# A mean-embedding projection on one Trainium2 core: tiles of users join the sweep over the weights three loads earlier

## What is computed

```python
valid = sequence_ids < emb_table.shape[0]          # ids 1024 x 200, table 12500 x 512
safe_ids = jnp.where(valid, sequence_ids, 0)
seq_emb = emb_table[safe_ids]
seq_emb = seq_emb * valid[..., None].astype(seq_emb.dtype)
denom = jnp.maximum(valid.sum(axis=1, keepdims=True).astype(seq_emb.dtype), 1.0)
user_repr = seq_emb.sum(axis=1) / denom
logits = user_repr @ proj_w + proj_b               # 512 x 12500, in fp32
```

## Time and profile before

| | |
|---|---|
| median of 3 runs | 706.61 us (704.24 to 707.12) |
| the profiled execution | 707.86 us, its span 706.1 us |
| TensorE busy | 638.2 us, 90% |
| VectorE, GpSimd, ScalarE busy | 396.0, 233.3, 147.6 us |
| granted TensorE clock, mean | 0.956 of full speed |
| DMA | 156.24 MB, mean 221 GB/s |
| read from HBM, written | 113.66 MB, 51.20 MB |
| chain that ended last | PE 76%, issue 9%, DVE 6%, DMA 4% |
| joins (first unit of tiles 1 to 7) | units 10, 22, 35, 51, 65, 81, 98 |

### The profile page before, as it was taken

The page is one execution under the profiler, slowest core; times in us unless marked ns, Lnnn a source line. Parts: engine busy times, 40 slices in busy tenths (PEclk is TensorE's granted clock), DMA queues, the critical chain, the costliest instruction groups (busy, mean ns, idle before and its releaser), DMA issues.

```text
span 706.1 us, 7456 instructions
## 1 busy us (share of the span) xinstructions
PE 638.2 (90%) x2627; PEld 491.2 (70%) x2627; DVE 396.0 (56%) x703; ACT 147.6 (21%) x173; POOL 233.3 (33%) x227
## 2 busy tenths in 40 slices
PE   1874797997989979987999999999999999999998
PEld 0323565765757747866878878888888888888886
DVE  7943843855937654967968754533333334434442
ACT  8402731623404202102002003211001111112110
POOL 6772747575663471763755400000000000000000
PEclk9985988999989988998999999999999999999999
DMA  9984987786876974985868816854545555566743
GB/s 316 357 256 121 336 307 223 248 295 213 288 217 187 313 251 156 299 258 175 313 220 267 296 73 206 285 171 162 165 146 174 161 186 167 165 219 193 211 146 109
DMA packets 75398, 156.24 MB, mean 221 GB/s; under 512 B 8007, under 2 KB 62738, under 8 KB 75354
## 3 DMA queue, kind: packets, MB, share of 16 engines
q1 hardware_dynamic: 58074, 108.25, 46.2%
q0 software_dynamic: 17280, 47.47, 22.0%
HBM read 113.66 MB, written 51.20 MB: 233 GB/s over the span
## 4 chain that ended last, share of the span: by engine, by line
PE 76%; issue 9%; DVE 6%; DMA 4%; ACT 2%; another core or an unknown queue 1%; POOLq 0%; POOL 0%; DVEq 0%; SPq 0%; ACTq 0%
PE acc L774 23%; PE acc L772 23%; PE acc L773 23%; PE turned L731 4%; DVE sums L522 3%; DMA rows<-in_L_rec_emb_table_dram,index 2%; DMA w_raw<-in_L_rec_proj_w_dram 1%; PE acc L776 1%; DVE w_lo L572 1%; PE turned L705 1%; PE turned L721 1%; ACT w_hi L398 1%; DVE mean L559 0%; DVE stage L584 0%
## 5 line engine op out<-in xcount | busy, mean ns | idle before, releaser
L772 PE MATMUL acc<-w_hi,mean_hi 128*128 128x500 f32 x800 | 328.9, 411 | 3.3 <-issue 3.1
L774 PE MATMUL acc<-w_hi,mean_lo 128*128 128x500 f32 x800 | 318.1, 398 | 1.2 <-issue 1.2
L773 PE MATMUL acc<-w_lo,mean_hi 128*128 128x500 f32 x800 | 316.2, 395 | 3.3 <-issue 3.2
L331 POOL DMA_INDIRECT rows<-in_L_rec_emb_table_dram,index x208 | 223.2, 1073 | 139.9 <-issue 71.9
L584 DVE TENSOR_TENSOR stage<-acc,bias_sb 128x500 f32<-128x500 f32 x149 | 100.6, 677 | 188.6 <-PE acc L774 178.7
L773 PEld LDWEIGHTS acc<-w_lo,mean_hi 128*128 128x128 f32 x800 | 154.3, 193 | 40.6 <-issue 8.5
L772 PEld LDWEIGHTS acc<-w_hi,mean_hi 128*128 128x128 f32 x800 | 154.4, 193 | 37.1 <-issue 8.1
L774 PEld LDWEIGHTS acc<-w_hi,mean_lo 128*128 128x128 f32 x800 | 153.5, 192 | 35.8 <-issue 4.4
L522 DVE SCALAR_TENSOR_TENSOR sums<-rows,mask,sums 128x512 f32<-128x512 f32 x159 | 119.6, 752 | 8.5
L398 ACT ACTIVATE w_hi<-w_raw 128x2000 fp32r<-128x2000 f32 x39 | 72.8, 1874 | 230.6 <-PE acc L774 210.8
L570 DVE TENSOR_TENSOR w_lo<-w_raw,w_hi 128x1000 fp32r<-128x1000 f32 x39 | 46.5, 1193 | 18.0 <-ACT w_hi L398 17.6
(11 more groups left out here) (92 smaller groups left out, 198.4 us busy)
## 6 DMA issues: line engine op xcount, KB each, us to landing
w_raw<-in_L_rec_proj_w_dram SPq DMA_DIRECT2D x39, 1000.0 KB
out_dram<-stage SPq DMA_DIRECT2D x72, 500.0 KB
out_dram<-stage SPq DMA_DIRECT2D x56, 250.0 KB
bias_sb<-in_L_rec_proj_b_dram SPq DMA_DIRECT2D x31, 250.0 KB
raw_at_hi<-in_L_rec_proj_w_dram SPq DMA_DIRECT2D x4, 1000.0 KB
raw_at_lo<-in_L_rec_proj_w_dram SPq DMA_DIRECT2D x4, 1000.0 KB
rows<-in_L_rec_emb_table_dram,index POOLq DMA_INDIRECT x208
ids_sb<-in_r_sequence_ids_dram SPq DMA_DIRECT2D x1, 700.0 KB, 4.6
```

Source lines behind the costliest of these rows:

```text
L331: return pool.indirect_dma_start(out=dst, out_offset=None, in_=table, in_offset=bass.IndirectOffsetOnAxis(ap=column, axis=0), bounds_check ...
L772: nc.tensor.matmul(bank, hi, high, start=k == 0, stop=False)
L773: nc.tensor.matmul(bank, hi, low, start=False, stop=False)
L774: last = nc.tensor.matmul(bank, lo, high, start=False, stop=k == K - 1 and r >= EARLY)
```

## The change

One line changes, the table of joins.

```diff
 def mean_embedding_projection(nc, ids, table, proj, bias, out, FAST=26,
-                              JOIN=(0, 10, 14, 17, 20, 22, 24, 26)):
+                              JOIN=(0, 7, 11, 14, 17, 19, 21, 23)):
```

## The result

The changed kernel takes 716.14 us (713.04 to 718.37, four runs), the kernel before, with one run more, 705.42 us. The ratio is 1.0139, with a 95% interval of 1.0102 to 1.0177: slower by 1.4%. I had forecast slower, 710.7 us against 706.61, which is 0.6%. The direction is right, the size, 4.1 us, is under half of the measured 10.7, and 716.14 lies 0.1 us over the upper end of the range. The profiled execution of the change took 718.37 us, 10.5 us more than that of the kernel before.

What follows compares the result with a forecast made beforehand. TensorE's units bound the last stretch; a chain of gathers, splits and waits bounds stage 1. Units +7.3 us less 3.2 us from an earlier join gave +4.1 us: 710.7 us against 706.61, range 701 to 716 us.

Steps and rivals of the forecast that it cites:

- The units at the end: Two more units in the last stretch cost 5.47 us, one more in stage 7 costs 1.85 us: together +7.3 us.
- what moves is the landing: Stage 1: TensorE's first gathered column lands 4.1 us sooner; with 0.86 us for a further sum, the join comes 3.2 us sooner.
- the middle of two bounds: TensorE's first column in stage 1 takes 5.9 us to land, between 4.40 and 7.38; join 4.7 to 1.7 us sooner.
- The further sum: Stage 1: the last gathers wait for two columns behind the split, not one, which costs 0.86 us.
- Stages 2 to 6 at nothing: Stages 2 to 6 keep their unit counts and cost nothing, covered by the 49 us each takes anyway.
- over 3 us in sum as a sign of being wrong: Stages 2 to 6 differing by more than 3 us in sum would mean their time is not the cadence read in it.
- the cadence rival: TensorE's signals come late in a long gather run across stage 1, eating the landing's gain: +7.3 us, 713.9; chance 0.16.
- Some 49 us whatever the count: Stages 2, 3, 5, 6 and 7, with 12 to 17 units, each take about 49 us regardless of units.
- The traffic: Rival: DMA traffic sets stage 1; gathers come 8.4 us sooner and 3.9 us of waiting goes: -5.0 us, 701.6; chance 0.24.
- The stage 4 load: Rival: VectorE's 5.71 us wait for a late load's split in stage 4 is on the path: -1.6 us, 705.0; chance 0.18.

Runs made afterwards that it cites:

- first pair: Traces of the kernel before and the change from the recorded result, 705.42 and 716.14 us, ratio 1.0139.
- second pair: Both kernels run again unchanged for their traces: the kernel before 661.42 us; the change 665.61 us against 661.12, ratio 1.0075.
- the kernel with more raw buffers: Kernel before with four raw buffers used up to load 18 in place of 15: 661.72 us against 660.56, ratio 1.0014.
- the joins from load 11: Kernel before with joins at loads 0, 11, 15, 18, 21, 23, 25, 27: 658.44 us, ratio 0.9963; with four raw buffers up to load 19, 654.91 us.

## Why the prediction was right and wrong

**The units at the end: right.** Forecast +7.3 us (5.47 and 1.85); measured +8.0 in the first pair of traces and in the second (2.4 and 5.6). The small rest is in stage 7, where 0.79 us of TensorE's waiting was still there with a unit more, so that only some 0.1 us of it was filled. The mean is made three units before the join and so moves with the units.

**Stage 1: the mechanism right, the number in part by luck.** The step "what moves is the landing" was forecast at 3.2 us by the middle of two bounds. In the second pair the join moved by 3.3 us. But TensorE's first column landed at 72.7 in place of 75.6, 2.9 us sooner and not 4.1. The further sum did cost what it should (4.69 us from the split to the last gathers in place of 3.84). The unit and the split behind the landing were 0.5 us faster, and the last two columns landed 0.8 us faster after their issue; neither was in the sum. And stage 1 of one order of work differs by 0.9 to 1.9 us from trace to trace. In the first pair the landing moved by 3.5 us, the mean by 3.7 and the join by 7.0; the other 3.3 us are the late take-up of the turning at 117.31, which the changed kernel had less of (ScalarE took it up at 110.79, and from the mean to the join it was 7.1 us and not 10.3).

**Stages 2 to 6 at nothing: the step that failed in the recorded result.** It measured +9.4 us in the first pair of traces, 7.1 of it in stage 2, and +0.5 in the second pair. The prediction had named over 3 us in sum as a sign of being wrong, and it came. In the first pair there are stops in which ScalarE takes up a finished unit 1.7 to 14.0 us late, in both kernels, at different places. In stage 2 they cost both kernels TensorE's waits at the turning and the list, the change 2.9 us more; the pauses between TensorE's matmuls, 2.4 us more, only lie beside such a stop. The forecast named late signals under the cadence rival and gave it 0.16. That rival's sum, +7.3, is nearer to the measured 10.7, but its place was not right: the loss ate the gain in stage 2, and not in stage 1. What causes the stops stays open. They are not a property of a long run of gathers, since the second pair has longer runs and none of them. Instruction loading is no likely cause either: the traces have 21 and 23 packets of it in both pairs.

**The reading behind it was wrong too.** "Some 49 us whatever the count" was taken from the first trace, and from a list that left out stage 4, with 58.89 us for 16 units. Where the signals came in time, stages 3 and 4 take 40.1 and 49.1 us for 13 and 16 units with TensorE busy throughout. There the cover of these stages was not a cadence but TensorE's own unchanged work, and the term was nothing for a different reason than the one I gave.

**The rivals.** The traffic (0.24) is refuted in its size: in the second pair the join came 3.3 us earlier, not 8.4. In the first it came 7.0 us earlier, and 3.2 of that is the waiting ahead of the join (3.9) which this rival had added. The stage 4 load (0.18) is refuted by the kernel with more raw buffers. It was a real mechanism in stage 3, though, as the joins from load 11 showed.

## What to carry to other kernels

A unit of the bound engine is free only where that engine waits, so moving a join is a trade: the full price of a unit at the end against what the gathers give back at the front, and the latter has to be worked out along the chain to the landing, not guessed from the count. When a table of joins is moved, look for what else is numbered by it: here a raw buffer's wait slid from a stage that could hide it into one that could not, and mending that was worth 3.0 us, as much as the joins from load 11 alone (2.7). A join can also change which unit a split waits for, and so open or close a ring of waits. And before a stage's time is called a cadence, ask whether the bound engine works through it or stands.

## What the hardware showed that I had not expected

The same kernel took 703 to 707 us in one set of runs and 659 to 665 us in another, with the same instructions. Stages 2, 3 and 4 have 49.5, 49.2 and 58.9 us in the one and 43.4, 40.1 and 49.1 in the other, while a unit of the last stretch takes 2.73 us in both. The difference of two kernels was 1.4% in the one and 0.75% in the other. The difference begins ahead of the first unit, which starts at 64.8 us in the one and at 53.5 in the other. What differs between the sets I can't say from the traces; the 661 us came on three chips, and the record names none for the slower set. The granted clock has a mean of 0.956 and of 0.990, and TensorE is busy for 638.2 and 622.6 us, so some 16 of the 48 us between the spans are slower matmuls and the rest is waiting. In the slower set, TensorE's own matmuls of one unit came apart by up to 1.75 us (stage 4 of the change), with no wait between them in the program.
